# Denominators gathered by tokens for the reciprocals, with a new order on ScalarE, other PSUM banks, and other places for one quad of scores and some copies

## The reference

```
x  = L0_attn_x                       # 16 x 256 x 128, float32
xn = layernorm(x)
x  = x + favor(xn) + local_ffn(xn)   # layer 0
xn = layernorm(x)
x  = x + attention(xn) + moe(xn)     # layer 1

favor:     q, k = exp(features) of 16 heads with 32 features each, causal sums over time
           num = sum_j<=t (q_t . k_j) v_j ;  den = sum_j<=t (q_t . k_j) ;  attn = num / den
           then output projection, residual, layernorm with gamma and beta
local_ffn: two times (shift, q/k/v of 8 heads x 64, l2-norm of q and k, rotary,
           softmax over a window of 64 tokens back, output projection,
           shift, layernorm, gated unit with gelu)
attention: 16 heads x 8, full softmax over 256 keys:  out = (exp(s - max) v) / sum exp(s - max)
moe:       8 experts of width 256, the best two by router, one shared expert, silu gates
```

## Time and profile before

| | |
|---|---|
| time, median of 3 runs | 2227.73 us (2225.33 to 2232.55) |
| the profiled execution, its own time | 2232.31 us |
| its span, first to last instruction | 2230.5 us |
| mean granted TensorE clock, share of full speed | 0.941 |
| busy: PE / PEld / DVE | 1846.4 us (83%) / 1070.3 us (48%) / 1322.2 us (59%) |
| busy: ACT / POOL | 776.0 us (35%) / 272.5 us (12%) |
| read from and written to HBM | 12.06 MB, 2.36 MB |

### The profile page before, as it was taken

One profiled execution on the slowest core, in us unless ns is written; L12 is line 12 of the kernel. 1 busy time (PEld: TensorE's weight loads), 2 busy tenths in 40 slices (PEclk: granted clock), 3 DMA queues, 4 the chain that ended last, 5 costly groups with the idle time before them and its releaser, 6 DMA issues.

```text
span 2230.5 us, 43273 instructions
## 1 busy us (share of the span) xinstructions
PE 1846.4 (83%) x18116; PEld 1070.3 (48%) x18116; DVE 1322.2 (59%) x2712; ACT 776.0 (35%) x1441; POOL 272.5 (12%) x222
## 2 busy tenths in 40 slices
PE   1788898888888888888988879788898888988877
PEld 1355444554454544545445455354444554444644
DVE  1566457675476654766547655656556665476644
ACT  0322343323432335223352333522443324523234
POOL 0101102101011011010210101101111101021010
PEclk9999899999998999989999999999999999999889
DMA  4000200002000020000200011000200002000020
GB/s 174 1 6 2 29 2 11 1 2 29 2 11 1 2 29 7 6 1 6 25 7 7 2 16 15 6 6 2 27 5 6 6 2 29 2 6 1 2 29 7
DMA packets 27476, 29.77 MB, mean 13 GB/s; under 512 B 3524, under 2 KB 25844, under 8 KB 26740
## 3 DMA queue, kind: packets, MB, share of 16 engines
q1 hardware_dynamic: 27284, 27.01, 6.3%
HBM read 12.06 MB, written 2.36 MB: 6 GB/s over the span
## 4 chain that ended last, share of the span: by engine, by line
PE 50%; DVE 28%; ACT 8%; SPq 6%; issue 4%; DMA 4%; POOL 0%; ACTq 0%; DVEq 0%
SPq L430 5%; PE bank L726 5%; PE bank L948 4%; DMA phi<-parts 4%; PE bank L938 3%; PE bank L758 3%; PE bank L923 3%; DVE ls L1444 2%; DVE ftm L1370 2%; DVE parts L1380 2%; PE bank L1037 2%; DVE lmx L1432 2%; PE bank L961 2%; DVE lc L1426 2%; PE bank L664 2%
## 5 line engine op out<-in xcount | busy, mean ns | idle before, releaser
L1605 DVE TENSOR_REDUCE amx<-bank 128x2 f32<-128x512 f32 x256 | 163.0, 685 | 69.5 <-PE bank L961 69.5
L1593 DVE TENSOR_TENSOR mh<-bank,silu 128x512 f32<-128x512 f32 x144 | 98.8, 691 | 149.8 <-PE bank L938 112.3
L1209 ACT ACTIVATE silu<-bank 128x512 f32<-128x512 f32 x144 | 84.2, 597 | 268.8 <-PE bank L923 256.7
L948 PEld LDWEIGHTS bank<-w_mw,mh 128*128 128x128 f32 x1152 | 144.8, 201 | 27.1 <-issue 27.1
L923 PE MATMUL bank<-xn2T,w_mw 128*128 128x512 f32 x288 | 153.1, 657 | 0.0
L948 PE MATMUL bank<-w_mw,mh 128*128 128x128 f32 x1152 | 151.7, 287 | 0.0
L1624 DVE RECIPROCAL ftm<-bank 128x512 f32<-128x512 f32 x16 | 53.7, 3357 | 165.2 <-PE bank L1044 165.2
L664 PE MATMUL bank<-hT,w_wqkv 128*128 128x512 f32 x256 | 119.0, 602 | 17.2 <-ACT hT L1069 11.0
L1432 DVE TENSOR_REDUCE lmx<-bank 128x4 f32<-128x512 f32 x128 | 79.5, 684 | 87.3 <-PE bank L726 87.3
L1444 DVE RECIPROCAL ls<-bank 128x256 f32<-128x256 f32 x64 | 112.1, 1751 | 23.8 <-PE bank L778 23.8
L466 POOL TENSOR_TENSOR lc<-lc,ls 128x512 f32<-128x512 f32 x32 | 41.0, 1280 | 679.7 <-DVE lc L1402 679.7
(11 more groups left out here) (283 smaller groups left out, 3682.4 us busy)
## 6 DMA issues: line engine op xcount, KB each, us to landing
phi<-parts SPq DMA_DIRECT2D x96, 64.0 KB
lc<-parts SPq DMA_DIRECT2D x96, 64.0 KB
w_mw<-in_mw SPq DMA_DIRECT2D x3, 1152.0 KB
x_in<-in_x SPq DMA_DIRECT2D x8, 256.0 KB, 2.7
out<-res SPq DMA_DIRECT2D x8, 256.0 KB, 2.3
w_wqkv<-in_wqkv SPq DMA_DIRECT2D x1, 1536.0 KB
w_w<-in_w SPq DMA_DIRECT2D x1, 682.0 KB
mh<-in_rotary SPq DMA_DIRECT2D x1, 512.0 KB
```

Source lines behind the costliest of these rows:

```text
L948: last = mm(bank_of("final")[:, t], mh[:, (2 * q + i) % 4, t], W["mw2"][:, ORDER[q], i, :], start=(q == 0 and j == 0 and i == 0), stop=Fal ...
L1209: A(silu[:, n % 2, :], bank_of("moe_g", n)[:], ACT.Silu).then_inc(sem["moe_silu"], 1)
L1593: V.tensor_tensor(mh[:, n % 4, :], bank_of("moe_u", n)[:], silu[:, n % 2, :], ALU.mult).then_inc(sem["moe_h"], 1)
L1605: V.tensor_reduce(amx[:, 2 * b:2 * b + 2, h], bank_of("att_max", n)[:].rearrange("p (t k) -> p t k", t=2), AX.X, ALU.max).then_inc(sem["at ...
```

## The change

- `den` is now 128x8. `favor_den` and `att_den` take the `heads` block as the stationary operand and `den` as the moving one, four times for each sequence, so that tokens come to lie on partitions and the 32 denominators of each (4 blocks x 8 heads) side by side. DVE takes the reciprocal of 128x32 numbers (`quot`) and copies each 16 times into `ftm`; PE transposes `ftm` back (`spread_quotients`, new steps `favor_rows` and `att_rows`), and DVE multiplies with that bank. In the local loop DVE does `favor_quotients` where the old reciprocal stood and the product behind n = 0; PE does `favor_rows` at n = 1.
- `favor_project` moves from n = 3 to n = 2. Quad 7's scores move behind `"raws"` and its sums behind `"sums"`.
- Banks: ring `"rows"` for the maxima's transposes is [3, 7, 3, 6] and was [4, 7, 5, 6]; `loc_sT` visits its four banks in the order 1, 2, 0, 3; one early value goes to bank 5.
- DVE copies the unshifted half of `hT` (features 0 to 63) that ACT copied before, in both layers and between them. `input_moments` of the next turn moves ahead of the wait for `glu_mean`.
- ACT: tables are placed by tiny activations (Gelu after the local exponentials, Exp after both gated units, Silu after part 1, Exp after the last gates). After part 1 come the gates, the second early value, `route_T`, the attention's values, the first `widen`, and only then part 2. The next turn's `hT` is copied before `xnT`.
- PE: only one early value stands before the transposes of `xn2`; the second follows the attention's v product. POOL makes part 3 behind the first expert's product.

```diff
-    "x_kept": 1, "xnT": 1, "hT": 4, ...
+    "x_kept": 1, "xnT": 1, "hT": 3, ...
-    den = np.zeros((P, P))
-    den[p // 16 * 16 + 8, p] = 1
+    den = np.zeros((P, 8))
+    den[np.arange(8) * 16 + 8, np.arange(8)] = 1
...
-                    (0, "mean"): 4, (0, "var"): 5, (0, "gain"): 6, (1, "sums"): 7}
+                    (0, "mean"): 4, (0, "var"): 5, (0, "gain"): 6, (1, "raws"): 7}
-                    (0, "var"): 4, (0, "gain"): 5, (0, "out"): 6, (1, "nmT"): 7}
+                    (0, "var"): 4, (0, "gain"): 5, (0, "out"): 6, (1, "sums"): 7}
...
-        RINGS = {..., "rows": [4, 7, 5, 6], ...}
+        RINGS = {..., "rows": [3, 7, 3, 6], ..., "late": [5]}
...
+                    if q == 1:
+                        pool.wait_ge(sem["att_part2"], now("att_part2", 1))
+                        nc.gpsimd.tensor_tensor(parts[:, :, 2, :], arest, parts[:, :, 1, :],
+                                                ALU.subtract).then_inc(sem["att_part3"], 1)
...
                 def favor_den(b):
                     pe.wait_ge(sem["favor_sums"], now("favor_sums", b + 1))
-                    mm(bank_of("favor_pv", b)[:], W["den"][:], heads[:, b, :], start=True, stop=True).then_inc(
-                        sem["favor_den"], 1)
+                    for i in range(4):
+                        last = mm(bank_of("favor_pv", b)[:, 8 * i:8 * i + 8], heads[:, b, i * P:(i + 1) * P], W["den"][:],
+                                  start=True, stop=True)
+                    last.then_inc(sem["favor_den"], 1)
+
+                def spread_quotients(o):
+                    for i in range(4):
+                        last = mm(o[:, i * P:(i + 1) * P], ftm[:, i, :], I[:],
+                                  start=True, stop=True)
+                    return last
+
+                def favor_rows(b):
+                    pe.wait_ge(sem["favor_rec"], now("favor_rec", b + 1))
+                    spread_quotients(bank_of("favor_pv", b)).then_inc(sem["favor_rows_ps"], 1)
...
-                        for i in range(4):
+                        for i in (1, 2, 0, 3):
                             pe.wait_ge(*freed("loc_sT", 4 * k + i))
...
                         if n == 0:
                             favor_den(l)
-                        if l == 1 and n == 3:
+                        if n == 1:
+                            favor_rows(l)
+                        if l == 1 and n == 2:
                             favor_project()
...
+                    A(warm[:], W["ident"][:, 0:1], ACT.Gelu)
                     for b in range(G):
                         t = slice(b * SEQ, (b + 1) * SEQ)
                         act.wait_ge(sem["loc_x"], now("loc_x", 2 * l + b + 1))
-                        A(hT[0:64, b, 0:SEQ], xB[0:64, t], ACT.Copy).then_inc(sem["glu_h"], 1)
                         A(hT[64:P, b, 1:SEQ + 1], xB[64:P, t], ACT.Copy).then_inc(sem["glu_h"], 1)
...
                 A(parts[:, :, 0, :], aqk, ACT.Copy).then_inc(sem["att_part1"], 1)
-                act.wait_ge(sem["att_rest"], now("att_rest", 1))
-                A(parts[:, :, 1, :], arest, ACT.Copy).then_inc(sem["att_part2"], 1)
-                act.wait_ge(sem["att_v_ps"], now("att_v_ps", 1))
-                act.wait_ge(sem["favor_pv"], now("favor_pv", 8))
-                spread_values("att_v")
+                A(warm[:], W["ident"][:, 0:1], ACT.Silu)
...
                 gates(0)
+                if it + 1 < TURNS:
+                    early_value(it + 1, 1)
                 act.wait_ge(sem["route_T_ps"], now("route_T_ps", 1))
                 A(wT, bank_of("route_T")[0:3 * EX, 0:256].bitcast(BF16), ACT.Copy).then_inc(sem["route_T"], 1)
+                act.wait_ge(sem["att_v_ps"], now("att_v_ps", 1))
+                act.wait_ge(sem["favor_pv"], now("favor_pv", 8))
+                spread_values("att_v")
                 widen(1)
+                act.wait_ge(sem["att_rest"], now("att_rest", 1))
+                A(parts[:, :, 1, :], arest, ACT.Copy).then_inc(sem["att_part2"], 1)
...
+                A(warm[:], W["ident"][:, 0:1], ACT.Exp)
                 if it + 1 < TURNS:
                     queries(it + 1)
...
+                def quotients(s, o):
+                    link(V.reciprocal(quot[:, s, :], o[:, 0:32]))
+                    return V.tensor_copy(ftm[:].rearrange("p t (h r) -> p (t h) r", r=16),
+                                         quot[:, s, :].unsqueeze(2).broadcast_to([P, 32, 16]))
...
                 def favor_out(b):
-                    share = ftm[:].rearrange("p t d -> p (t d)")
-                    dve.wait_ge(sem["favor_den"], now("favor_den", b + 1))
-                    link(V.reciprocal(share, bank_of("favor_pv", b)[:]))
-                    V.tensor_tensor(heads[:, b, :], heads[:, b, :], share, ALU.mult).then_inc(sem["favor_att"], 1)
+                    dve.wait_ge(sem["favor_rows_ps"], now("favor_rows_ps", b + 1))
+                    V.tensor_tensor(heads[:, b, :], heads[:, b, :], bank_of("favor_pv", b)[:], ALU.mult).then_inc(
+                        sem["favor_att"], 1)
...
-                    favor_out(l)
+                    favor_quotients(l)
                     for n in range(4):
...
+                        if n == 0:
+                            favor_out(l)
...
+                        dve.wait_ge(sem["loc_x"], now("loc_x", n + 1))
+                        V.tensor_copy(hT[0:64, b, 0:SEQ], xB[0:64, t]).then_inc(sem["loc_lo"], 1)
+
+                    if l == 0 and it + 1 < TURNS:
+                        input_moments(it + 1)
...
                 for b in range(G):
-                    share = ftm[:].rearrange("p t d -> p (t d)")
                     dve.wait_ge(sem["att_den"], now("att_den", b + 1))
-                    if b:
-                        dve.wait_ge(sem["att_o"], now("att_o", 1))
-                    V.reciprocal(share, bank_of("att_pv", b)[:]).then_inc(sem["att_rec"], 1)
-                    dve.wait_ge(sem["att_rec"], now("att_rec", b + 1))
-                    V.tensor_tensor(heads[:, b, :], heads[:, b, :], share, ALU.mult).then_inc(sem["att_o"], 1)
+                    quotients(1, bank_of("att_pv", b)).then_inc(sem["att_rec"], 1)
+                    dve.wait_ge(sem["att_rows_ps"], now("att_rows_ps", b + 1))
+                    V.tensor_tensor(heads[:, b, :], heads[:, b, :], bank_of("att_pv", b)[:], ALU.mult).then_inc(sem["att_o"], 1)
```

More of the change, by code:

```diff
@@ L245, in build @@
                   6: ((9,), (10,), (11,)), 7: ((12,), (13,), (14, 15))}
-        RINGS = {"short": range(0, 6), "long": range(6, 8), "quad": range(0, 4), "norm": range(4, 8), "rows": [4, 7, 5, 6], "wide": [4, 5, 6, 0], "wide1": [4, 5, 7, 0],
-                 "five": range(0, 5), "seven": [0, 1, 2, 3, 4, 7, 5], "acc": [6], "tail": [7, 5], "spare": [7]}
+        RINGS = {"short": range(0, 6), "long": range(6, 8), "quad": range(0, 4), "norm": range(4, 8), "rows": [3, 7, 3, 6], "wide": [4, 5, 6, 0], "wide1": [4, 5, 7, 0],
+                 "five": range(0, 5), "seven": [0, 1, 2, 3, 4, 7, 5], "acc": [6], "tail": [7, 5], "spare": [7], "late": [5]}
         RING_OF = {"favor_pv": "long", "att_pv": "tail", "loc_ss": "long",
@@ L257, in job @@
         def job(name, k, freed_by, count, ahead=0):
-            ring = ("quad", "wide", "quad", "wide1")[k // 4] if name == "loc_max" else "long" if (name, k) in LONG else RING_OF[name] if name in RING_OF else "short"
+            ring = "late" if (name, k, ahead) == ("loc_v", 1, 1) else ("quad", "wide", "quad", "wide1")[k // 4] if name == "loc_max" else "long" if (name, k) in LONG else RING_OF[name] if name in RING_OF else "short"
             i = RINGS[ring][turns_of[ring] % len(RINGS[ring])]
@@ L335, in build @@
             job("glu_out", l, "x1" if l else "glu_x", 1)
-        job("xnT", 0, "hT", 2, ahead=1)
-        for j in range(EARLY):
-            job("loc_v", j, "loc_v", j + 1, ahead=1)
+        job("xnT", 0, "xnT", 1, ahead=1)
+        job("loc_v", 0, "loc_v", 1, ahead=1)
         job("xn2T", 0, "xn2T", 1)
@@ L343, in build @@
         job("att_v", 0, "att_v", 1)
+        job("loc_v", 1, "loc_v", 2, ahead=1)
         def weight_job(q):
@@ L534, in favor_query, with early_value @@
                 mm(o[:], W["fw"][:, i, :], xnT[:], start=True, stop=True).then_inc(sem["favor_qk_ps"], 1)
-            def early_values(it):
+            def early_value(it, j):
                 now, prior, freed = counters(pe, it)
                 pe.wait_ge(sem["hT"], now("hT", 2))
-                for j in range(EARLY):
-                    pe.wait_ge(*freed("loc_v", j))
-                    b, t = divmod(j, 2)
-                    mm(bank_of("loc_v", j)[:], hT[:, b, t * P:(t + 1) * P],
-                       W["wqkv"][:, 0, 2 * INNER:3 * INNER], start=True, stop=True).then_inc(sem["loc_v_ps"], 1)
+                pe.wait_ge(*freed("loc_v", j))
+                b, t = divmod(j, 2)
+                mm(bank_of("loc_v", j)[:], hT[:, b, t * P:(t + 1) * P],
```

(31 more changed lines are left out.)

39 lines of the change are left out of this document (22 added, 17 removed).

## The result

The changed kernel takes 2261.8 us (median of 4 runs, 2257.8 to 2265.4) against 2227.7 (2225.3 to 2232.6): ratio 1.015 (95% interval 1.0126 to 1.0174), 34.1 us slower. The forecast was slower by 16. The direction and the places were right, the sum was half of what came. Of the two profiled executions one spans 2260.3 us, the other 2230.5: 29.8 us to explain.

A forecast was written before the change was run, and what follows sets the result against it. Bound by the chain of waits, half TensorE and more than a quarter VectorE. Terms: +24 (8x), -7 (7x), -1.1 for the last denominators, so +16: 2243.5 us against 2227.7; own range 2233 to 2256, 8 in 10 within 2202 to 2262.

The forecast's parts named there:

- The favor product's wait: Softmax loops: second maxima rows wait for the favor product's bank; first loop +1.9 us (0 to +2.5), 8 times.
- half clock long: Rival, slower, chance 0.09: half clock after the DMA stop lasts twice as long, also transposes before it; 2260 us.
- Second loop, 1.2 instead of 1.9: Second layer's softmax loop: same +1.9 us wait, less an earlier favor_project's gain; +1.2 (-0.7 to +2), 8 times.
- Quad 7: Second layer: values 0 and 1 wait for the last two squares, ahead of quad 7 and sums; +1.7 us (0 to +2), 8x.
- Input moments: Moved into the wait for the mean, ending PE's 1.26 us idle for the root; -1.3 us (-1.0 to -1.5), 7x.
- Half copies and the second gated unit: Parallel half copies between layers -0.6 us; second layer's centring and early Gelu table -0.7 (-0.4 to -1.7); each 8x.
- Stretch before the part copy: One early value leaves PE and ACT, gain half counted because of half clock; -0.5 us (-1.2 to +0.3), 7x.
- ACT's new order and the DMA stop: Behind the part copy: 4.28 us stop goes, DMA wait grows to 5 to 8, half clock follows; +1.5 (0 to +3), 7x.
- Exp table and attention: Attention: table load moves into idle time, -0.8 us (-0.5 to -1.3); transposes between pairs 14 and 15, +0.3; each 8x.
- Turn change: Last attention denominators to PE's map: shorter reciprocal chain, but transposes delay raw products; -0.7 us (0 to -1.4), 7x.
- Waits met: Rival, faster, chance 0.14: waits for favor_att and the squares are covered, their 4.8 us go; 2199 us.
- Clock: Rival, faster, chance 0.20: each turn settles on the short 266.3 us kind, two half-clock stretches vanishing; 2220 us.

The follow-up runs named there:

- product first: Changed kernel with VectorE's favor product right behind its quotients, ahead of the first denominators' reciprocal of each softmax loop: 2202.0 us, ratio to before 0.9874.
- experiment 7: Changed kernel with favor product ahead of the reciprocal and quad 7 at its old places (2187.5 us), plus favor_project back at n = 3: 2196.0 us.
- experiment 6: Changed kernel with favor product ahead of the reciprocal and quad 7 at its old places (2187.5 us), plus ScalarE's old order behind the first part copy: 2179.7 us.
- the last version: Changed kernel with favor product ahead of the reciprocal, quad 7 back, long reciprocals in the softmax loops, ScalarE's old order behind the first part copy: 2161.5 us.

## Why the prediction was right in direction and wrong in size

**The favor product's wait, 16 times: place and length right, price wrong.** The prediction had the waiting instruction, the bank and 1.9 us; the trace has 2.1. It then priced the wait alone. Behind each such stop PE ran at the lower clock, 1.6 us a loop, in six of eight first loops and in seven of eight second loops. Over the run that clock is 9.7 us in the first loops and 11.3 in the second. The step that failed is "+1.9 (0 to +2.5)" and its sister "+1.2": 24.8 us forecast for both loops, 43.0 measured, and 53.5 gone once the wait was taken away. The text itself named the mechanism, but priced it for one stop only, that of the DMAs, because the earlier trace rows showed it there. In the earlier trace rows each stop of PE should have had a clock price, at least as an upper end; the bounds of this step left it out, and the rival "half clock long" looked at the DMA stop alone. The trace of before held a hint that a stop of this size can bring the half clock. In its first turn the DMA stop was 1.84 us, less than turn 7's 4.26, and the 16 matmuls behind it took 3.68 us, longer than turn 7's 3.06:

```profile
275.83 0.39 PE L961 MATMUL bank<-lc,phi 48*128 48x256 bf16 x4 [1.84 <-DMA phi<-parts]
276.15 3.68 PE L948 MATMUL bank<-w_mw,mh 128*128 128x128 f32 x16
```

Two other sizes in the loops were off, one against the other. Four short products and four transposes in place of the old product delay the second maxima rows by 1.3 us in the first loop and 1.7 in the second (product first against before), where 1.05 was taken; and the first maxima rows come 1.6 and 2.1 us a turn earlier, where 1.1 was taken.

**The sum over all terms.** The loops missed by 18.2 us, the stretch before the part copy by 5.6. Against them the experts came 6.7 lower than forecast and the input moments 4.6. That the whole missed by 14 in the profiled executions and not by more is this cancelling, not accuracy.

**Second loop, 1.2 instead of 1.9.** The credit for the earlier favor_project was real: 0.76 in a usual turn (experiment 7) against 0.7.

**Quad 7.** Forecast 1.7 a turn, measured 1.92. The timeline of the second layer (changed kernel) shows the steps as foretold against the earlier trace rows: values, the first of them with a wait for the last square but one, quad 7's scores, and `sums` directly behind them.

```profile
445.23 2.32 PE L694 MATMUL bank<-w_wqkv,hT 128*128 128x512 f32 x4 [1.15 <-ACT silu L1147]
...
447.48 0.71 PE L599 MATMUL bank<-phi 32*128 32x256 f32 x8
...
448.35 0.62 PE L674 MATMUL bank<-lsq,w_sumrow 128*32 128x512 f32 x2
```

What it cost beyond that, the clock in the second loop, was not in the sum.

**Input moments.** Forecast 1.3, measured 1.5 when undone and 13.7 over the run in its stretch instead of 9.1. PE's wait at the earlier trace rows is gone; in six turns the gain is 2.0 to 2.3 us, 0.8 to 1.0 more than its 1.26. The difference goes with the clock: the mean granted clock of this stretch was 0.81 in the seven turns before and is 0.89 in those six; in the one turn where it is still 0.80 the gain is 0.8.

**Half copies and the second gated unit.** 0.66 a turn between the layers (forecast 0.6), 6.1 us for the second unit (5.6): right.

**Stretch before the part copy.** Forecast -0.5 with an upper end of +0.3, measured +0.2 to +0.4 in seven turns. The transposes of xn2 now stand where those of turn 7 stood in the earlier trace rows, at half clock: 1.08 us.

```profile
788.95 1.08 PE L521 MATMUL bank<-w_ident,ftm 128*128 128x128 f32 x4 [1.88 <-DVE ftm L1352]
```

The loss that the prediction had counted half came whole: the mean granted clock from the second gated unit's output product to the part copy fell from 0.90 to 0.80 in six of these turns.

**ACT's new order and the DMA stop.** The stop at the earlier trace rows went and the one at the stacks grew, to 2.3 to 5.6 us where "near 7" was foretold. Where it was 5.3 us, PE came back at half clock, longer than the earlier trace rows had it: 16 matmuls in 3.78 us, and the ones behind too.

```profile
1099.59 0.61 PE L985 MATMUL bank<-lc,phi 48*128 48x256 bf16 x4 [5.33 <-DMA phi<-parts]
1100.13 3.78 PE L972 MATMUL bank<-w_mw,mh 128*128 128x128 f32 x16
1103.84 1.03 PE L985 MATMUL bank<-lc,phi 48*128 48x256 bf16 x8
```

Three turns lost 2.7 to 3.0 us by it. Three others won 0.7 to 3.6; there the first maximum, which waits for the stacks, came 23.0 to 24.2 us after the part copy's start, against 26.3 to 26.7 in the three that lost. So the stretch shows +3.8, not +10.5, and yet undoing the order gave 8.9 and 13.1 us there: the term was of about the right size. What it was set against, 5.1 us that this stretch gains over before with the old order too (4.5 of them in the first turn), no term had. The sentence on the Trainium skill (TensorE: Matmul & The Clock Gate, section "HAM oscillation — how this bites in real kernels"), that waits for DMAs throttle the engine and the work behind pays, held at the DMA stop in seven of eight turns of the changed kernel (the 16 matmuls took 2.71 to 3.78 us) and not in the one with a stop of 2.5 us (2.05 us). The softmax loops showed the like behind a wait for DVE, of which I had not asked it.

**Exp table and attention.** -4.0 forecast, -3.9 measured. Turn change: 0.61 a turn (0.7). That the sum of the attention agrees is chance: it holds +3.4 of the last turn, whose experts came 3.6 earlier; the seven other turns have -0.4 to -0.6 (three) and -1.4 (four) where -0.5 was forecast.

**Rivals.** "Waits met" had priced both order waits gone at 2199. With the product's wait alone gone it is 2201 to 2202, with quad 7 back at its old places too 2187.5. So the rival's condition was the one that decides; its price was 11.5 us too high, and that 2199 lies near 2202 is chance. "Clock" did not happen in the changed kernel (turns of 269.7 to 275.9 us, none at 266, mean granted clock 0.940), but much of it does once the product's wait is gone (0.951; an estimate from it: 0.941 to 0.951 is about 47 us less at the lower level, half of it time, near the 24 that this rival had).

## What to carry to other kernels

When a planned wait gets longer, price it twice: the wait, and the work behind it at the lower clock; here 2.1 us of wait cost 3.7 in 13 of 16 loops. Before gathering or shrinking an operation, look at what its engine's time lies beside: at their own places the short reciprocals won 4.3 us where PE waited for them (attention; 8.9 in the time) and lost 13.0 where it did not (loops; 18.5 in the time), by PE's extra transposes. Where a bank's ring puts an operand under a product of another engine, swap two entries of the ring first; that one edit was worth 61 us here.

## What the runs showed of the hardware that I had not expected

- The lower clock doesn't follow from one stop alone: in the second loops the same 2.1 us wait was followed by 2.4 to 2.5 us for 32 matmuls in seven of eight turns of the changed kernel, and by 1.38 us in all eight when quad 7 stood at its old places.
- The length of a stop alone doesn't tell what follows it. In the changed kernel a stop of 5.3 us for DMAs was followed by 16 matmuls in 3.78 us and one of 2.5 us by full clock (2.05 us), but one of 2.3 us, in the last turn, by 3.55 us; in experiment 6 stops of 3.0 and 3.1 us were followed by 2.05 us.
- From the start of the part copy to the first use of the stacks, behind the 24 stack DMAs, it took from 23.0 to 26.7 us in the turns of one program, with the same issues. No run here tells why.
- Edits whose gain was work or wait added up (2161.5 us against 2161 expected for the last version, from two terms measured alone, with executions up to 11 us apart from it); two edits that both removed the same half clock gave 74 us together and 91 alone.
